# Attention on one core: the last two diagonal key blocks of each half as one unit

## The reference, cut to what matters

```python
q = rope((resid @ Wq) as 32 heads of 32); k, v: 8 key heads of 32
qg = q.reshape(B, 8, 4, T, 32)
att = einsum('bhgqd,bhkd->bhgqk', qg, k) / sqrt(32)
att = where(causal, att, -inf)                # T = 1024
probs = softmax(att, axis=-1)
ctx = einsum('bhgqk,bhkd->bhgqd', probs, v)
out = ctx (2 x 1024 x 1024) @ Wo
```

## Time and profile before

| | |
|---|---|
| median of 3 runs | 1619.24 us (1617.63 to 1626.55) |
| the profiled execution | 1616.91 us |
| its span, first to last instruction | 1615.2 us, mean granted clock 0.982 |
| PE busy | 1551.4 us, 96% |
| DVE, POOL, ACT busy | 940.3 us (58%), 623.4 us (39%), 588.1 us (36%) |

### The profile page before, as it was taken

The page is one execution under the profiler, slowest core; times in us unless marked ns, Lnnn a source line. Parts: engine busy times, 40 slices in busy tenths (PEclk is TensorE's granted clock), DMA queues, the critical chain, the costliest instruction groups (busy, mean ns, idle before and its releaser), DMA issues. The chain is left out here.

```text
span 1615.2 us, 26661 instructions
## 1 busy us (share of the span) xinstructions
PE 1551.4 (96%) x9392; PEld 1193.9 (74%) x9392; DVE 940.3 (58%) x2707; ACT 588.1 (36%) x1201; POOL 623.4 (39%) x403
## 2 busy tenths in 40 slices
PE   7999997999999789999999999999988999999999
PEld 7999996788888655555555555555458999999998
DVE  6644553646463387888888788788427333333333
ACT  4333333212120126666666656666623121111110
POOL 1322222434343306767776666667722010010100
PEclk9999999999999969999999999999999999999999
DMA  6332233333322444333333434441353131313220
GB/s 225 120 121 99 101 133 125 124 118 117 105 96 80 140 94 100 92 87 87 87 99 87 100 92 108 107 98 35 86 192 122 53 105 53 105 53 102 73 71 40
DMA packets 152311, 162.75 MB, mean 101 GB/s; under 512 B 41744, under 2 KB 110608, under 8 KB 151920
## 3 DMA queue, kind: packets, MB, share of 16 engines
q1 hardware_dynamic: 123600, 137.37, 29.4%
q10 hardware_dynamic: 28592, 23.86, 4.5%
HBM read 104.05 MB, written 61.90 MB: 103 GB/s over the span
## 5 line engine op out<-in xcount | busy, mean ns | idle before, releaser
L1460 ACT ACTIVATE at_probs<-ps 128x512 f32<-128x512 f32 (+3 forms) x768 | 324.3, 494 | 141.8 <-PE ps L1376 139.4
L1533 DVE CUSTOM_DVE_ANT_0 ps<-ps,at_score_mask 128x512 f32<-128x512 f32 (+3 forms) x512 | 290.9, 618 | 37.9 <-PE ps L1365 34.4
L323 POOL TENSOR_TENSOR f_x_ring<-f_x_ring,f_half_bias 128x1024 f32<-128x1024 f32 x32 | 79.4, 2483 | 321.8 <-DVE f_h L580 321.3
L1376 PE MATMUL ps<-at_qs,at_ks 98*128 98x512 f32 (+3 forms) x528 | 192.7, 391 | 7.8 <-ACT at_probs L1460 5.4
L1365 PE MATMUL ps<-at_ks,at_qs 96*128 96x512 f32 (+3 forms) x528 | 176.2, 369 | 11.3 <-DMA at_ks<-scr_k_hi 10.6
L1376 PEld LDWEIGHTS ps<-at_qs,at_ks 98*128 98x128 f32 x528 | 97.6, 193 | 116.4 <-ACT at_probs L1460 90.1
L1391 PE MATMUL ps<-at_probs,at_vs 128*32 128x512 f32 (+3 forms) x1536 | 162.9, 496 | 0.2 <-POOL at_probs L1289 0.2
L1311 POOL TENSOR_TENSOR at_added<-at_added,at_probs 128x2048 f32<-128x2048 f32 x32 | 147.8, 4619 | 2.3
L1533 DVE CUSTOM_DVE_ANT_0 ps<-ps,at_score_mask,at_part_max 128x128 f32<-128x128 f32 (+3 forms) x256 | 133.7, 557 | 13.1 <-issue 10.7
L48 PE MATMUL ps<-f_wt_hi,f_hT_hi 128*128 128x400 f32 (+1 forms) x384 | 132.4, 345 | 4.9 <-DVE f_wt_lo L641 4.9
L48 PE MATMUL f_ps<-f_wt_hi,f_hT_hi 128*128 128x400 f32 (+1 forms) x384 | 133.7, 348 | 3.2 <-DVE f_hT_lo L584 3.2
(11 more groups left out here) (159 smaller groups left out, 3148.7 us busy)
## 6 DMA issues: line engine op xcount, KB each, us to landing
at_qs<-scr_q_hi SPq DMA_DIRECT2D x20, 512.0 KB, 6.1
f_x_ring<-in_L_attn_resid SPq DMA_DIRECT2D x16, 512.0 KB, 3.6
x<-f_x_ring SPq DMA_DIRECT2D x16, 512.0 KB, 2.7
early<-x SPq DMA_DIRECT2D x16, 512.0 KB, 3.5
scr_q_hi<-qkv_rope_hi ACTq DMA_DIRECT2D x32, 256.0 KB, 2.0
scr_q_lo<-qkv_rope_lo ACTq DMA_DIRECT2D x32, 256.0 KB, 2.3
scr_ctx_hi<-at_ctx_hi SPq DMA_DIRECT2D x32, 256.0 KB, 2.2
scr_ctx_lo<-at_ctx_lo SPq DMA_DIRECT2D x32, 256.0 KB, 2.5
```

What stands on the lines that cost most here:

```text
L323: pool.tensor_tensor(x_ring[:, u, :], x_ring[:, u, :], half_bias[:], ALU.add).then_inc(bias_added, 1)
L1376: pe.matmul(score_ps[(u * G + g) % BANKS][:, 0:z - a], ks[:, nm, j * P:(j + 1) * P], qs[nm][0:KROWS + 2, half, g, a - half * HALF:z - half ...
L1460: act.activation(probs[:, u % PROBS, g, 0:z - a], score_ps[(u * G + g) % BANKS][:, 0:z - a], ACT.Exp, scale=SCALE).then_inc(exp_done, 1)
L1533: dve.tensor_tensor_reduce(out=src, in0=src, in1=mask, scale=1.0, scalar=part_max[:, g, own] if c else -3.0e38, op0=ALU.add, op1=ALU.max, ...
```

## The change: what it does

The last two key blocks of each half (j = 2 and 3, j = 6 and 7), 256 and 128 queries wide, become one unit of 384 columns. A head has ten units, three for half 0 and seven for half 1, with widths 512, 384, 384, and five times 512, 384, 384. A merged unit still has two score matmuls for each `g`, into neighbouring columns of one bank, with one signal behind the second; one exponential of 384 columns for each `g`; one mask over both triangles; and its eight context products in one run, behind the half's sums in the last unit. The ring of six `probs` buffers is now indexed by the running number of the unit, since ten is no multiple of six. The dealing of the row products goes over ten units, and the hand-written places are renumbered. The fourth item of unit 0 stays the turn of half 1, whose first unit is now unit 3 instead of 4.

```diff
-    ADDED = range(4, 8)
+    ADDED = range(3, 7)
...
-        units = [(half, j) for half in range(2) for j in range(QH * (half + 1))]
+        units = [(0, (0,)), (0, (1,)), (0, (2, 3))] + [(1, (j,)) for j in range(NQ - 2)] + [(1, (NQ - 2, NQ - 1))]
         NU = len(units)
-        LAST = {QH - 1: 0, NU - 1: 1}
+        H0 = QH - 1
+        LAST = {H0 - 1: 0, NU - 1: 1}
...
+        def blocks(u):
+            half, js = units[u]
+            out, at = [], 0
+            for j in js:
+                a = max(j * P - half * HALF, 0)
+                out.append((j, slice(a, HALF), slice(at, at + HALF - a)))
+                at += HALF - a
+            return out
...
-        room = [queries(u)[1] - queries(u)[0] + 1200 for u in range(NU)]
+        room = [width(u) + 1200 for u in range(NU)]
...
-                tile = probs[:, u % PROBS, :, 0:P]
+                count = len(units[u][1])
+                tile = probs[:, (NU * n + u) % PROBS, :, :].rearrange("p g (b n) -> p g b n", b=2)[:, :, 0:count, 0:P]
...
-                                   pattern=[[0, G], [1, P]], channel_multiplier=-1).then_inc(mask_done, 1)
+                                   pattern=[[0, G], [0, count], [1, P]], channel_multiplier=-1).then_inc(mask_done, 1)
...
-                    if u in (3, 4, 6):
-                        add(n, (5, 6, None, 7)[u - 3])
-                    if n and u == 8:
+                    if u in (2, 3, 5):
+                        add(n, (4, 5, None, 6)[u - 2])
+                    if n and u == 7:
                         low(n - 1, 1)
+                    if u == 8:
+                        divide(n, 0)
+                    if u == 7:
+                        low_wo(n)
                     if u == 9:
-                        divide(n, 0)
-                    if u == 8:
-                        low_wo(n)
-                    if u == 11:
                         low(n, 0)
...
-                pe.matmul(score_ps[(u * G + g) % BANKS][:, 0:z - a], ks[:, nm, j * P:(j + 1) * P], qs[nm][0:KROWS + 2, half, g, a - half * HALF:z - half * HALF],
-                          start=True, stop=True).then_inc(scores_done, 1)
+                for j, at, cols in blocks(u):
+                    last = pe.matmul(score_ps[x % BANKS][:, cols], ks[:, nm, j * P:(j + 1) * P], qs[nm][0:KROWS + 2, half, g, at],
+                                     start=True, stop=True)
+                last.then_inc(scores_done, 1)
...
-                    if n and u == 5:
+                    if n and u == 4:
                         high(n - 1, 1)
-                    if u == 7:
+                    if u == 6:
                         high_wo(n)
-                    if u == 10:
+                    if u == 9:
                         high(n, 0)
...
-                    if u == 5:
+                    if u == 4:
                         reciprocal(n, 0)
```

More of the change, by code:

```diff
@@ L1110, in attention_stage, with width @@
         ctx_stored = [sem(f"ctx_stored{h}") for h in range(2)]
-        units = [(half, j) for half in range(2) for j in range(QH * (half + 1))]
+        units = [(0, (0,)), (0, (1,)), (0, (2, 3))] + [(1, (j,)) for j in range(NQ - 2)] + [(1, (NQ - 2, NQ - 1))]
         NU = len(units)
-        LAST = {QH - 1: 0, NU - 1: 1}
[L1115 to L1123, removed]
+        H0 = QH - 1
+        LAST = {H0 - 1: 0, NU - 1: 1}
+        LAST_OF = (H0 - 1, NU - 1)
+        APART = (range(H0), range(ADDED[-1] + 1, NU))
+        def blocks(u):
[6 more added lines that the diff above has]
+            return out
+        def width(u):
+            return blocks(u)[-1][2].stop
+        diagonal = [u for u in range(NU) if units[u][1][0] >= units[u][0] * QH]
         rows = [("row", i, g, c) for i in range(NQ) for c in range(i // QH + 1) for g in range(G)]
@@ L1164, in attention_stage @@
         early = rows[OPEN + 8:OPEN + 20]
[L1165 to L1168, removed]
+        for u in range(H0):
+            placed[0, u] = of(0, early[4 * u:4 * u + 4])
+        for u, items in enumerate(spread([TURN_A] + rows[at_a:], weight[at_a:], room[H0:])):
+            placed[0, H0 + u] = of(1, items)
         for n in range(1, NG):
@@ L1180, in attention_stage @@
             for u in range(NU):
-                if n == 0 and u in (0, QH):
-                    for key in BEFORE[u // QH] + [key for part in BETWEEN[u // QH] for key in part]:
+                if n == 0 and u in (0, H0):
+                    for key in BEFORE[u // H0] + [key for part in BETWEEN[u // H0] for key in part]:
                         number[key] = len(number)
@@ L1193, in ahead @@
             if u + AHEAD < NU:
-                return None if n == 0 and QH - AHEAD <= u < QH else (n, u + AHEAD)
+                return None if n == 0 and H0 - AHEAD <= u < H0 else (n, u + AHEAD)
             return (n + 1, u + AHEAD - NU) if n + 1 < NG else None
@@ L1306, in add @@
                     pool.wait_ge(unit_done, NU * n + NU)
-                    first = probs[:, ADDED[0] % PROBS, :, :]
+                    first = probs[:, (NU * n + ADDED[0]) % PROBS, :, :]
                 else:
@@ L1310, in add @@
                     first = added[:]
-                pool.tensor_tensor(added[:], first, probs[:, u % PROBS, :, :], ALU.add).then_inc(added_done, 1)
+                pool.tensor_tensor(added[:], first, probs[:, (NU * n + u) % PROBS, :, :], ALU.add).then_inc(added_done, 1)
             def low_wo(n):
@@ L1368, in scores @@
             def scores(n, u, g):
[L1370 to L1373, removed]
+                half, js = units[u]
+                nm, x = n % RING, NU * G * n + (u * G + g)
+                if js[0] == 0 and g == 0:
                     pe.wait_ge(rows_loaded[half], ROW_LOADS * n + (ROW_LOADS + 16))
-                pe.wait_ge(exp_done, NU * G * n + (u * G + g + 1))
-                pe.matmul(score_ps[(u * G + g) % BANKS][:, 0:z - a], ks[:, nm, j * P:(j + 1) * P], qs[nm][0:KROWS + 2, half, g, a - half * HALF:z - half * HALF],
-                          start=True, stop=True).then_inc(scores_done, 1)
+                pe.wait_ge(exp_done, x + 1)
+                for j, at, cols in blocks(u):
+                    last = pe.matmul(score_ps[x % BANKS][:, cols], ks[:, nm, j * P:(j + 1) * P], qs[nm][0:KROWS + 2, half, g, at],
+                                     start=True, stop=True)
+                last.then_inc(scores_done, 1)
             def products(n, u):
-                half, j = units[u]
-                a, z = queries(u)
-                at = slice(a - half * HALF, z - half * HALF)
+                half, js = units[u]
                 if u in diagonal:
@@ L1387, in products @@
                     pe.wait_ge(exp_done, NU * G * n + (G * (u + 1) + BANKS))
-                if j == 0:
+                if js[0] == 0:
                     pe.wait_ge(ctx_copied, 2 * n + (half + 1))
-                for g in range(G):
-                    last = pe.matmul(ctx_ps[g * DH:(g + 1) * DH, at], vs[:, n % RING, j, :], probs[:, u % PROBS, g, 0:z - a],
-                                     start=j == 0, stop=u in LAST)
+                for j, at, cols in blocks(u):
+                    for g in range(G):
+                        last = pe.matmul(ctx_ps[g * DH:(g + 1) * DH, at], vs[:, n % RING, j, :],
+                                         probs[:, (NU * n + u) % PROBS, g, cols], start=j == 0, stop=u in LAST and j == js[-1])
                 last.then_inc(unit_done, 1)
@@ L1398, in sums @@
                 pe.wait_ge(slot_read, q + 1)
-                pe.wait_ge(mask_done, len(diagonal) * n + (QH * (half + 1)))
+                pe.wait_ge(mask_done, len(diagonal) * n + (H0 * (half + 1)))
                 out = slot_ps[q % SLOTS]
@@ L1405, in sums @@
                 for u in APART[half]:
[L1406 to L1409, removed]
+                    for j, at, cols in blocks(u):
+                        for g in range(G):
+                            last = pe.matmul(out[g * DH:(g + 1) * DH, at], ones[:], probs[:, (NU * n + u) % PROBS, g, cols],
+                                             start=u == 0, stop=u in LAST and j == units[u][1][-1])
                 last.then_inc(slot_filled, 1)
@@ L1414, in _ @@
                 for u in range(NU):
-                    if n == 0 and u in (0, QH):
-                        half = u // QH
+                    if n == 0 and u in (0, H0):
+                        half = u // H0
                         for m, it in BEFORE[half]:
@@ L1452, in exps @@
             def exps(n, u, g):
[L1453 to L1456, removed]
+                x, cols = NU * G * n + (u * G + g), slice(0, width(u))
+                if g == 0 and NU * n + u >= PROBS:
+                    m, v = divmod(NU * n + u - PROBS, NU)
+                    act.wait_ge(unit_done, NU * m + (NU + 1 + (v if v in ADDED else LAST_OF[units[v][0]])))
                     if v in ADDED:
-                        act.wait_ge(added_done, ADDS * n + (ADDS * earlier + max(v - ADDED[0], 1)))
```

(17 more changed lines are left out.)

## The result

| | before | after |
|---|---|---|
| median of 4 runs of each on one chip | 1621.68 us | 1675.47 us |
| ratio, 95% interval | | 1.034 [1.031, 1.037] |
| profiled execution | 1616.91 us | 1675.56 us |
| its span | 1615.2 us | 1673.8 us |
| mean granted clock of TensorE | 0.982 | 0.953 |

The changed kernel is 3.4% slower, 58.65 us on the two profiled executions. The forecast was 1654 us, slower. The direction and the place were right; the size was 22 us too small.

The account below looks back on a forecast made before the run. TensorE was taken to bound the attention stage. Per head -0.5 - 1.0 + 3.2 + 1.0 = +2.7, times 15 is +40; with head 0's gain of 1.5 and the last head's -2, +37 on 1616.9: 1654 us, range 1630 to 1676.

Parts of the forecast that it names:

- groups and bank waits: TensorE, per head: two fewer groups of context products save 0.5 us, vanished waits for a score bank save 1.0.
- TensorE ready for half 1's scores: Start of a head: TensorE reaches half 1's scores about 3.4 us after the head's first scores.
- rows there: Start of a head: half 1's row-maximum DMAs land 6.6 to 6.7 us after the head's first scores.
- idle: TensorE stands from 3.4 to 6.6 us waiting for the rows: +3.2 us in 15 heads, bounds 1.6 and 4.5.
- clock: Behind the row wait TensorE's clock falls, losing 1.4 us in two heads of three: +1.0 per head, bounds 0 and 3.
- last head, GpSimd's mask: Last head: half-1 sums wait 2.40 us for GpSimd's last mask, which now comes earlier: -2 us.
- rival A: Same stall at the row transfer, but TensorE keeps 2.4 GHz: +22 us, 1639 us; chance 0.22.
- rival B: The clock falls in each of 15 heads, losing 2.5 us each time: +60 us, 1676 us; chance 0.15.
- The chain: Head start: ScalarE copy and `high`, GpSimd `low`, SyncE stores, then row DMAs; stores at 3.6, row DMAs 4.8 us.
- What was charged at nothing: Score matmuls, fewer exponentials and the merged mask (between 0.65 and 2.6 us, needed some 6 us later): 0 each.
- Rival D: VectorE becomes the bound, losing at most 1 us a head: 1633 us without any transfer stall; chance 0.03.
- Rival C: Row transfer stays hidden, only the gains count: -26 us, 1591 us, chance 0.08; balanced form 1615 to 1619, chance 0.07.

Follow-up runs that it names:

- a4: Kernel after, but the first unit of half 1 leaves out the two row-maximum rows and their wait (part of the computation omitted): 1599.02 us, 0.989 of before.
- a3: Kernel after with ten superfluous 512-column matmuls filling TensorE's wait for the rows in heads 1 to 14: 1647.80 us, 1.018 of before.
- a1: Kernel after with SyncE issuing the next head's half-1 row DMAs ahead of the store of half 0: 1650.39 us, 1.020 of before.
- a2: Kernel after with `divide(n, 0)` and `high(n, 0)` one unit earlier: 1641.26 us, 1.014 of before.
- b1: Kernel before with only `high(n, 0)` moved into the last unit, nothing merged: 1650.90 us, 1.020 of before.
- b3: Kernel after with only half 1's blocks merged, half 0 keeping four units, and `high(n, 0)` in the unit before the last: 1600.87 us, 0.988 of before.

## Why the prediction was right in its mechanism and wrong in its size

Per steady head, with a4 and a3 as the scale: 40.92 = 35.44 (merged units) + 2.71 (idle) + 2.77 (clock).

| step | forecast | measured |
|---|---|---|
| groups and bank waits | -1.5 | -1.33 (a4) |
| TensorE ready for half 1's scores | 3.4 behind the head's first | 880.67 - 877.25 = 3.42 |
| rows there | 6.6 | 883.38 - 877.25 = 6.13 |
| idle | +3.2 | +2.71; 2.96 in the mean of 15 heads |
| clock | +1.0 (1.4 in two of three heads) | +2.7 in all 15 (a3) |
| sum of a head | +2.7 | +4.15 |
| last head, GpSimd's mask | 2.40 to 0.4 | 1.06 + 0.25 left |

**The term that failed is the clock**, as the prediction put it: "I take 1.4 in two heads of three, +1.0." It took the 1.4 from the one stretch of 2.7 us at 0.50. That reading is right, for the clock was back soon behind it (first line below, 0.93), but not every low stretch is as short. After the change the clock stays low for some 6 us, half of which would be 3.0 of TensorE's work; a3 measured 2.7. The trace of before had a nearer row, which the prediction passed over: behind a wait of 2.68 at 1228.89, in the feed-forward part, the clock stood at 0.50 for 5.4 us, and half of that is 2.7.

```profile
1179.60:1181.00 1.40, 1.40 (x24) 0.58 (x20) 0.00 (x0) 0.00 (x0) 0.49 (x1) 0.93 0.00 0
1228.90:1234.30 5.40, 5.40 (x19) 5.04 (x20) 4.30 (x14) 1.23 (x2) 0.00 (x0) 0.50 0.00 2
```

```profile
1228.89 0.67 PE L48 MATMUL ps<-f_wt_hi,f_hT_hi 128*128 128x360 f32 x1 [2.68 <-DVE f_wt_lo L641]
```

And the clock fell in every head, not in two of three. Two of three was a choice between a gap of 2.40 that lost the clock and one of 2.80, at 37.31, that kept it; the second was also the evidence for rival A. That it kept the clock was chance: in a1, whose edit doesn't touch that place, the same wait, 2.78 long, lost it. The matmul behind it took 0.47 where it had taken 0.33, and the clock stood at 0.50.

```profile
38.43 0.47 PE L390 MATMUL f_ps<-ident,f_low_s 128*128 128x128 f32 x1 [2.78 <-DVE f_low_s L610]
```

```profile
38.00:41.00 3.00, 2.57 (x8) 2.55 (x9) 2.45 (x11) 2.01 (x4) 0.00 (x0) 0.50 0.00 0
```

What came is rival B (1676), which was given 0.15; that its time fits this well is partly luck, for the prediction shows no row for its 2.5 a head. The difference in the clock's term, 1.7 x 15 = 26 us, is more than the whole error of 22. The waits were smaller than forecast (44.3 us in the fifteen heads against 3.2 x 15 = 48, -4), the gains too (0.2 x 15, +3); the 3 us that remain, the other way, were not taken apart. The Trainium skill (TensorE: Matmul & The Clock Gate, HAM oscillation) tells of a clock lost in every tile of a kernel whose waits on a DMA are long, some 3 to 5 us there. The kernel after agrees, 15 of 15 with waits of 2.69 to 3.95; in a2, with waits of 1.64 to 2.93, it was 11 of 15.

**The chain was right link by link, but for one.** Copy at +0.14, `low` done at +2.61 (forecast 2.56), stores issued at +3.57 (3.6), row DMAs at +4.83 (4.8): SyncE's order decided, as said. The landing of 1.9 was added to the end of the issue; the view counts it from the start (881.49 + 1.89 = 883.38). That is the 0.5 by which the idle was too large. By the same count the rows of before land at 818.98 + 1.9 = 820.9, half a microsecond ahead of the scores at 821.42, so "with nothing to spare" was a little too strict for that head. In four other heads of the same trace the scores did wait, 0.35 to 0.69, and b1, with 0.53 of waiting for one call moved, shows too how little the slack is.

**What was charged at nothing cost nothing.** The merged mask takes 1.10 where two took 0.65 each, and its products wait for it once in the stage, in the last head (1.1 in the table of waits). Of the waits for a bank in the units named one is left in a steady head, 0.21 in step 0 (878.94), and that is what the forecast of 0.2 for that step said. Rival D has nothing for it: VectorE is busy 72.6 of 100 us, less than before. Rival C (faster, by a hidden transfer) is what a4 and b3 are, 1599 and 1601: the gain was there, and the place of half 1's first scores, with the late calls, took it.

**Open.** In a few heads, largely the same ones in all kernels, the rows land later (waits of 3.23 to 3.95 instead of 2.71 in the kernel after). In those four heads of the kernel after one issue of the chain takes SyncE 0.90 to 1.82 us (at 757.10, 922.32, 1125.77 and 1167.83), where 0.51 to 0.59 is usual; why was not found.

## What to carry to other kernels

Before two steps are merged, ask which transfers are hidden behind the number of steps and not behind their length: here half 0's merge brought about 0.3 us a head and took away a step, for which the scores then waited 1.65 (a2), and 2.71 with the calls late. Merge where no such cover hangs on it (b3 kept three quarters of the gain with none of the loss). And a wait that leaves TensorE idle in each round is to be priced at its length plus what the clock may cost: here 2.7 us of idle time cost another 2.7.

## What the runs showed of the hardware that was not expected

Equal waits do not have equal prices. Of the nine waits of 1.65 us in a2 six lost the clock and three kept it, as did those of 1.88 in a1 (six and three); a wait of 2.12 in a2 kept it, and one of 1.24 in b1 lost it, while the seven of 0.52 to 0.56 there all kept it. All fifteen from 2.69 up lost it. What TensorE did ahead of the waits is the same work in each head, so the length of the wait alone doesn't decide; what does was not found. A fall has no fixed price either: in a2 a head with a wait of 1.65 took 37.12 with the clock kept, and 38.59 or 40.03 with the clock lost. Superfluous matmuls in the wait kept the clock in each of the twelve heads in which they left at most 1.02 us idle (a3), and made the kernel some 26 us faster than the kernel after.

The Trainium skill (TensorE: Matmul & The Clock Gate, What's actually happening) says that the chip watches TensorE's activity in a window that runs freely and isn't set by the kernel. Unequal prices of equal waits would fit that; no run here was made to test it, so it stays a possibility.
